# A deformable convolution with a ternary residual block: the head reordered, weight preparation moved, taps of the offset convolution levelled, x1 loaded two chunks ahead

## The reference

```
x = x + deform_conv(gn(x), w_off, b_off, w_conv)
x = x + block(gn(x), w1, gamma1, beta1, w2, gamma2, beta2)

deform_conv: om = conv3x3(y, w_off) + b_off        # 27 channels: 18 offsets, 9 masks
             for each of 9 taps: sample y bilinearly at the shifted place, times sigmoid(mask)
             out = sum over taps and channels with w_conv (256 x 256 x 9)
block:       out1 = relu(bn(conv3x3(y, ternary(w1))))
             out2 = bn(conv3x3(out1, ternary(w2)))
             out  = relu(out1 + out2)
ternary(w):  w - mean(w); -1 below min + third, +1 above max - third, else 0
```

## Time and profile before

| | |
|---|---|
| median of 3 runs | 2930.91 us (2930.48 to 2938.26) |
| the profiled execution | 2936.16 us, its span 2934.3 us |
| head, to VectorE's first chunk | 117.5 us |
| batch 0, chunks 0 to 7 | 574.0 us |
| batches 1 and 2 | 1054.9 us |
| batch 3 and the last chunk's end | 506.1 us |
| tail | 166.9 us |
| second block | 514.9 us |

### The profile page before, as it was taken

The page is one execution under the profiler, slowest core; times in us unless marked ns, Lnnn a source line. Parts: engine busy times, 40 slices in busy tenths (PEclk is TensorE's granted clock), DMA queues, the critical chain, the costliest instruction groups (busy, mean ns, idle before and its releaser), DMA issues. The chain is left out here.

```text
span 2934.3 us, 38779 instructions
## 1 busy us (share of the span) xinstructions
PE 2442.2 (83%) x12442; PEld 1692.3 (58%) x12442; DVE 2234.0 (76%) x4734; ACT 1275.2 (43%) x2181; POOL 1367.5 (47%) x1262
## 2 busy tenths in 40 slices
PE   4288888888999999999999998889887677999930
PEld 3144444444566566556566665555555677999930
DVE  6667777777888888888888887888786664666566
ACT  3244444445644445555555444444443123233245
POOL 1345554555655555556556555666652003333300
PEclk9699999999999999999999998999998888999975
DMA  7788888899999999999999999999995112111179
GB/s 248 270 292 301 317 304 303 311 348 353 332 360 354 360 351 351 342 329 363 337 361 363 343 330 325 345 347 343 342 343 218 50 61 70 53 60 52 44 278 408
DMA packets 277755, 826.29 MB, mean 282 GB/s; under 512 B 25692, under 2 KB 59484, under 8 KB 276964
## 3 DMA queue, kind: packets, MB, share of 16 engines
q0 software_dynamic: 165888, 604.05, 55.0%
q1 hardware_dynamic: 111716, 220.47, 21.7%
HBM read 738.95 MB, written 85.48 MB: 281 GB/s over the span
## 5 line engine op out<-in xcount | busy, mean ns | idle before, releaser
L447 POOL DMA_INDIRECT G<-pixel_pairs,quad_c x1152 | 1204.9, 1046 | 896.7 <-PE psT L1169 582.8
L961 DVE SCALAR_TENSOR_TENSOR G<-G,wts_c 128x256 f32<-128x256 f32 (+1 forms) x2304 | 1258.4, 612 | 217.5 <-DMA G<-pixel_pairs,quad_c 212.2
L1077 PE MATMUL psD<-ST,wconv 128*128 128x512 f32 x2304 | 1079.1, 613 | 0.0
L551 ACT ACTIVATE G<-G,wts_c 128x256 f32<-128x256 f32 x1152 | 490.5, 497 | 496.6 <-DVE G L961 496.5
L1077 PEld LDWEIGHTS psD<-ST,wconv 128*128 128x128 f32 x2304 | 434.6, 199 | 444.9 <-issue 444.9
L1169 PE MATMUL psT<-idn,G 128*128 128x128 f32 x2304 | 323.5, 286 | 218.8 <-ACT G L551 216.6
L607 ACT ACTIVATE ST<-psT 128x1024 f32<-128x1024 f32 x288 | 294.1, 1021 | 419.4 <-PE psT L1169 419.2
L1169 PEld LDWEIGHTS psT<-idn,G 128*128 128x128 f32 x2304 | 269.8, 146 | 314.7 <-ACT G L551 185.2
L1065 PE MATMUL psF<-pl,qw 128*128 128x256 f32 x1872 | 267.6, 298 | 35.7 <-DVE h1c L809 24.9
L1065 PEld LDWEIGHTS psF<-pl,qw 128*128 128x128 f32 x1872 | 244.2, 195 | 53.3 <-DVE h1c L809 21.2
L1046 PE MATMUL psA<-po,woff 128*64 128x512 f32 x864 | 253.2, 437 | 0.0
(11 more groups left out here) (214 smaller groups left out, 2241.0 us busy)
## 6 DMA issues: line engine op xcount, KB each, us to landing
xx<-in_x SPq DMA_DIRECT2D x56, 512.0 KB, 4.3
pixel_pairs<-yT SPq DMA_DIRECT2D x104, 256.0 KB, 7.2
G<-pixel_pairs,quad_c POOLq DMA_INDIRECT x1152, 6.6
x<-x1c SPq DMA_DIRECT2D x32, 512.0 KB
h<-h1c SPq DMA_DIRECT2D x32, 512.0 KB, 9.1
out<-h SPq DMA_DIRECT2D x16, 1024.0 KB, 17.3
xf<-x SPq DMA_DIRECT2D x24, 640.0 KB, 8.5
area<-h SPq DMA_DIRECT2D x24, 640.0 KB, 4.1
```

Source lines behind the costliest of these rows:

```text
L447: pool.indirect_dma_start(out=G[:, i % RING, :], out_offset=None, in_=tbl[d.b].rearrange("y x q c -> (y x) (q c)"), in_offset=bass.Indirec ...
L551: act.activation(g, g, ACT.Copy, scale=wts_c[:, d.p, i:i + 1]).then_inc(d_scaled, 1)
L961: dve.scalar_tensor_tensor(g[:, 0:w], g[:, w:2 * w], wts_c[:, d.p, q * NG + i:q * NG + i + 1], g[:, 0:w], ALU.mult, ALU.add).then_inc(d_ma ...
L1077: ins = pe.matmul(psD[:, oc, :], wconv[:, t, k, oc * 128:(oc + 1) * 128], ST[:, k % 3, t, :], start=(k == 0 and t == 0), stop=(k == TAPS - ...
```

## The change

It has five parts.

- SyncE's first loads: the two small constants that TensorE needs go first, then x of image 0, then the other constants. TensorE, ScalarE and VectorE no longer wait for all constants before they start; the offset weights are prepared after the moments (`offset_weights`).
- The head loses w1 (its 2.3 MB load and all work on it), the borders of tables 1 to 3, which go behind the last table write together with the load of w_conv, and the indices of chunk 1. The moments of image 1 read four buffers (all of xx) instead of two.
- w1 is loaded in six parts twice, once for its sums (VectorE at tap 3 of chunks 0, 3 and 4) and once for the comparison (chunks 6 and 7); its Winograd form is made at tap 7 of chunk 7.
- `O_TAPS` starts with one tap after k = 0 and ends after k = 4; `J_TAPS` moves to k = 5 to 8. The offset results of image s+1 are evacuated and turned one tap later, and both halves of their indices are made at k = 8. Those of image 0 are evacuated in the chunk behind, with the indices at k = 4 and 5.
- In the tail a chunk's load and `normalise` are done two chunks ahead. w2's sums are taken in chunks 4 and 5 of batch 3 from a load of their own; its ternary and Winograd forms are made by GpSimd in the tail. `load_w2`, `weight_sums` and `weight_limits` do for it what they do for w1.

```diff
-            xres, xz = xx[:, 0], [xx[:, 3], xx[:, 1]]
+            xres, xz = xx[:, 0], xx[:, 3]
...
+            w1_part = [xx[:, 1 + i].rearrange("p t x -> p (t x)")[:, 0:3 * C] for i in range(2)]
-            zero_sb = xf[:, 0, :, :, :].rearrange("p t h w -> p (t h w)")[:, 0:2 * C]
+            w2_part = [xo_flat[:, i * 3 * C:(i + 1) * 3 * C] for i in range(3)]
+            zero_sb = pl[:].rearrange("p q t r w -> p (q t r w)")[:, 3000:3000 + 2 * C].bitcast(F32)
...
-                    walk(eng, at, 5 if s == 0 else 3)
-            J_TAPS = {0: [0, 1], 1: [2, 3], 2: [4, 5], 3: [6, 7, 8]}
-            O_TAPS = {0: [0, 1, 2], 1: [3, 4], 2: [5, 6], 3: [7, 8]}
+                    walk(eng, at, 3 if 0 < s < NB - 1 else 5)
+            J_TAPS = {5: [0, 1], 6: [2, 3], 7: [4, 5], 8: [6, 7, 8]}
+            O_TAPS = {0: [0], 1: [1, 2], 2: [3, 4], 3: [5, 6], 4: [7, 8]}
...
+                def load_hz(r):
+                    if r >= 4:
+                        sp.wait_ge(z_stat, NR + CREDIT + r - 3)
+                    sp.dma_start(xx[:, r % 4], rows_of(x, 1, r * RC, RC)).then_inc(hz_load[r % 4], 16)
+
...
+                    for r in range(4):
+                        load_hz(r)
+                    load_j(Chunk(0, 2, 1, 0, False, False))
+                    sp.wait_ge(s_zero, 6)
+                    table_border(0, s_edge)
...
-                        if r == 1:
-                            sp.wait_ge(s_edge, 16 * 4 * NB)
-                            load_j(Chunk(0, 2, 1, 0, False, False))
-                        if 1 <= r < NR - 1:
-                            load_z(Chunk(1, r + 1, (r + 1) // 2, (r + 1) % 2, False, r + 1 == NR - 1))
-                        if r == 2:
-                            sp.dma_start(wconv[:].rearrange("p t k o -> p t (k o)"),
-                                         w_conv.rearrange("(t c) k o -> c t (k o)", c=128)).then_inc(s_wconv, 16)
...
+                        if r < 4:
+                            load_hz(r + 4)
+                        if r == 4:
+                            load_o(Chunk(1, 0, 0, 0, True, False))
+                    sp.dma_start(wconv[:].rearrange("p t k o -> p t (k o)"),
+                                 w_conv.rearrange("(t c) k o -> c t (k o)", c=128)).then_inc(s_wconv, 16)
+                    for b in range(1, NB):
+                        table_border(b, s_edge_rest)
+                    sp.wait_ge(z_stat, 2 * NR + CREDIT)
+                    load_w1(0)
...
-                    if f2:
+                    if f2 and (s < NB or f.first):
                         load_f(f2)
+                    if s == NB and f2 and not f2.last:
+                        load_f(f2.after())
...
+                        hold(sp, s_w2p, 3)
+                        load_w2(3)
...
+                    if s == 0 and d.is_row(6):
+                        sp.wait_ge(s_w1p, 8)
+                        load_w1(2)
...
+                        sp.wait_ge(s_w1p, 10)
+                        load_w1(4)
...
+                        for r, p0, done in ((0, 2, 2), (3, 4, 4), (4, 0, 6)):
+                            if d.is_row(r):
+                                sp.wait_ge(s_w1p, done)
+                                load_w1(p0)
...
+                def w2_ternary():
+                    pool.wait_ge(s_lim, 1)
+                    pool.wait_ge(s_wraw, 16)
+                    pool.tensor_scalar(above2, stage2, wall[:, 3:4], wall[:, 6:7], ALU.subtract, ALU.is_gt)
...
+                    g = [above2.rearrange("p (t y i) -> p t y i", t=CT, y=3)[:, :, y, :] for y in range(3)]
+                    both, minus = (stage2.rearrange("p (t y i) -> p t y i", t=CT, y=3)[:, :, y, :] for y in range(2))
+                    pool.tensor_tensor(both, g[0], g[2], ALU.add).then_inc(s_w2, 1)
...
+                    pool.tensor_scalar(minus, minus, 0.5, None, ALU.mult)
+                    pool.tensor_scalar(g[1], g[1], 0.5, None, ALU.mult).then_inc(s_tern, 1)
+
+                def emit(s, z, o, d, f, o2, f2, j, j2, fp, jp):
+                    if s == NB and f.first:
+                        w2_ternary()
...
-                            pool.wait_ge(s_edge, 16 * 4 * NB)
+                            pool.wait_ge(s_edge, 16 * 4)
...
+                        if f and f.first and not d and k == 1:
+                            planes_hi(s, f)
+                            normalise(f2, xf, f_load, sc1, bi1, f_y, None)
...
-                        if f2 and k == f_step(d, f):
+                        if f2 and d and k == f_step(d, f):
...
-                        if o and k == 4:
+                        if jp and k == 1:
+                            jt_om_evac(jp)
+                        if j and k == 1:
+                            jt_normalise(j)
+                        if jp and k == 3:
+                            jt_om_turned(jp)
+                        if o and k == 5:
                             om_evac(o)
...
+                    offset_weights()
                     dve.wait_ge(h_y, 2)
                     jt_split(j0, x_rows(0, 9))
-                    dve.wait_ge(s_w1, 48)
-                    weight_sums(0, raw1[0][3])
-                    take_stats(Chunk(1, 0, 0, 0, True, False))
-                    weight_sums(1, raw1[1][3])
-                    step(weight_sums(2, raw1[2][3]))
-                    weight_sums_ready(3)
+
...
+                        for t in range(CT):
+                            i = dve.bn_stats(st0[:, t, r, :], xx[:, r % 4, t, :])
...
-                    weight_extremes(0)
-                    weight_limits(0)
-                    compare_w1(0)
-                    take_stats(Chunk(1, 2, 1, 0, False, False))
-                    take_stats(Chunk(1, 3, 1, 1, False, False))
-                    compare_w1(1)
-                    compare_w1(2)
...
-                    winograd_w1()
-                    jt_split(j2, xf_rows(j2))
-                    jt_indices(j1, 0)
-                    jt_indices(j1, 1)
-                    for r in range(4, NR):
...
+                        if s == NB - 1 and k in (1, 3, 5) and (d.is_row(4) or d.is_row(5)):
+                            part = k // 2 + (3 if d.is_row(5) else 0)
+                            dve.wait_ge(s_w2l, 48 if d.is_row(4) else 96)
+                            weight_sums(part, w2_part[k // 2]).then_inc(s_w2p, 1)
...
-                        if o and k in (7, 8):
-                            o_indices(o, k - 7)
-                        if j and k in (7, 8):
-                            jt_indices(j, k - 7)
-                        if j2 and k == 7:
-                            jt_split(j2, xf_rows(j2))
+                        if o and k == 8:
+                            o_indices(o, 0)
+                            o_indices(o, 1)
+                        if j and k == 2:
+                            jt_split(j, xf_rows(j))
+                        if jp and k in (4, 5):
+                            jt_indices(jp, k - 4)
+                        if s == 0 and k == 3:
+                            for r, p0, loaded in ((0, 0, 32), (3, 2, 64), (4, 4, 96)):
+                                if d.is_row(r):
+                                    dve.wait_ge(s_w1, loaded)
+                                    for part in (p0, p0 + 1):
+                                        weight_sums(part, w1_part[part % 2]).then_inc(s_w1p, 1)
+                                    if r == 4:
+                                        dve.wait_ge(s_w1p, 6)
+                                        weight_sums_ready(6)
...
+                        if s == 0:
+                            for r, kk, p0, loaded in ((6, 1, 0, 128), (6, 6, 2, 160), (7, 6, 4, 192)):
+                                if d.is_row(r) and k == kk:
+                                    dve.wait_ge(s_w1, loaded)
+                                    compare_w1(p0)
+                                    compare_w1(p0 + 1)
+                        if s == 0 and k == 7 and d.is_row(7):
+                            dve.wait_ge(s_w1p, 12)
+                            winograd_w1()
...
                     if s == NB and f.first:
-                        dve.wait_ge(s_wraw, 16)
-                        step(weight_sums(0, stage2))
-                        weight_sums_ready(1)
...
+                    pe.wait_ge(s_const, 80)
+                    for r in range(3, 6):
+                        for tap in range(3 * (r - 3), 3 * (r - 2)):
+                            jt_conv(j0, tap)
+                        turn(r)
+                    turn(6)
                     jt_turn_om(j0)
...
+                    if s == 0 and d.is_row(5):
+                        pe.wait_ge(s_wtr, 2)
+                    if s == 0 and d.is_row(6):
+                        pe.wait_ge(s_lim1, 1)
...
+                            if k == 2 and jp:
+                                jt_turn_om(jp)
+                            if k == 6:
...
```

(27 more changed lines are left out.)

214 lines of the change are left out of this document (100 added, 114 removed).

## The result

| | before | after |
|---|---|---|
| median of 4 runs | 2934.59 us (2930.48 to 2940.38) | 2903.93 us (2900.94 to 2909.6) |
| the profiled execution, its span | 2936.16, 2934.3 us | 2900.94, 2899.2 us |

The ratio is 0.9898, with a 95% interval of 0.9880 to 0.9915. The direction was right; 2826 us was too fast by 78, and the result lies 42 us outside the range of 2797 to 2862.

A forecast was written before the change was run, and what follows sets the result against it. Batches 1 and 2 nearly fill TensorE, VectorE and DMA, batch 3 is DMA-bound; slack lies elsewhere. -40 - 26 + 0 + 7 - 46 = -105 on 2936.2 us gives 2831, the median 5.2 lower: 2826 us, range 2797 to 2862.

The forecast's parts named there:

- Head, -40: Start of the kernel: GpSimd starts at 70.1 us instead of 110.3, so -40 us; bounds -46 and -30.
- Batch 0, -26: Batch 0: levelled offset taps shorten chunks 1 to 5; sum 548 for 574 us, -26; bounds -42 and -5.
- a third shows: +7: Batch 0, chunks 6 and 7: of 21 us more VectorE work a third lengthens them, +7 us.
- Batches 1 and 2, 0: Batches 1 and 2: moved taps and index halves at tap 8 change the time by 0.
- the bounds that I gave: Batches 1 and 2: 1 us either way in each of 16 chunks.
- Same totals, other places: Batches 1 and 2: the work only moves between taps, its totals stay, so 0 us.
- The rival on late offsets: Batches 1 and 2: VectorE waits at tap 8, up to 7.3 us a chunk, batch 0 gains nothing: 2969 us; chance 0.03.
- Batch 3, +7: Batch 3: w2's second load costs 7 us, its sums are hidden or 8 us in part; bounds 0 and +15.
- Tail, -46: Tail: x1 two chunks ahead leaves TensorE the bound, six chunks at 12.2 us, -46 us; bounds -50 and -18.
- GpSimd's part: Tail: GpSimd's w2 passes take 19.9 us over two operands and 10 to 26 over one, from near 2284.
- ahead of the last matmul: Tail: GpSimd's w2 work ends between 2314 and 2331, before the last matmul.
- The first rival: Tail: GpSimd's SBUF passes stop VectorE's two-SBUF-operand plane operations; 28 us of gain lost, 2854 us; chance 0.23.

The follow-up runs named there:

- the early load: The changed kernel with the last two parts of w1 loaded ahead of chunk 7's table write in SyncE's queue, not behind it: 2900.53 us, one run.

## Why the prediction was wrong

**Head, -40: right, but for 3 us.** The rows show the steps as forecast: moments as x lands, then a queue that only writes and loads from 29.04 (forecast 28.7). Its writes and loads took 40.8 us instead of 37.6, and GpSimd starts 3.4 us later than forecast (73.5 for 70.1). No run undoes a part of the head by itself.

**Batch 0, -26: right in chunks 1 to 5, wrong at its end.** The step that failed is "a third shows: +7" for chunks 6 and 7. I counted VectorE's work on w1 and not a wait for its last load, which SyncE issues behind a wait of 25.9 us and a table write; VectorE stood 7.5 us for it. The chunks lost 17, and the early load gave 7.7 back in chunk 7; with it the two chunks still took 136.7 us, 11 above before for the 7 forecast. Chunk 0 took the full DMA (a share of 1.01 at 385 GB/s) and by its first multiply was still 6.6 us shorter (77.3 to 70.7).

**Batches 1 and 2, 0: wrong by 12 us,** within the bounds that I gave. "Same totals, other places" failed as a step: at a TensorE busy for 996 of 1055 us, the places cost too: with the older ones the batches took 1059.5 and 1061.2 us. The rival on late offsets named this place and asked for 5 us a chunk; it was 0.8, and by one profile most of it not from the indices that it blamed.

**Batch 3, +7: mis-sized, with the terms exchanged.** The sums, taken as hidden, cost about all of the 14 us: 18 reductions of 0.94 us, 17 us, on a VectorE that is busy for 50.4 of the 61 us of such a chunk before. The load, taken as the 7, cost nothing that one profile shows.

**Tail, -46: the main error, 44 of the 70 us between the forecast's 105 and the profile's 35.** Two things stood in the step on "GpSimd's part". Its ending "ahead of the last matmul" was taken as all that mattered, and the exclusion of VectorE given 0.23. And the passes were sized at 30 to 46 us and took 63.3: the four two-operand passes took 22.2 us for 19.9, near the forecast from the earlier trace rows (2.33 ns a column over 4608), but the comparison with two operations cost 3.45 ns (15.89 us for 4608), above my upper bound of 2.15. (VectorE worked beside these passes too, and no run has them alone, so how much of the 3.45 is theirs is open.) The first rival had the mechanism (an operation of the planes waits for a pass) and, with 28 us, the loss of the third chunk (27.23 us of TensorE's waiting). That this number fits is partly luck: it had all six operations of the planes wait, and only two did, for passes that were longer than thought. And GpSimd was still at work when the fourth chunk's planes came, and that chunk lost another 16.91. "SBUF — State Buffer" of the Trainium skill, section "Who interferes with whom", had named the effect, and the runs agree with it at every point they touch: a GpSimd pass that reads SBUF stretches a VectorE operation with both operands in SBUF (16.77 us for 2.50); the additions with one operand in PSUM keep their 0.41 us. My reason for giving it less weight, that a pass waiting for VectorE would cost nothing, counted only one of the two directions. That the gain of the two-ahead loads itself was right is shown by the tail of 97.3 us. From its first to its last matmul the forecast of -46 is 100 us (145.9 less 46; the 120 of the prediction counts from the end of the last deformable chunk). With GpSimd out and w2's limits ready, the chunks wait for next to nothing; the price is the 8 us by which w2's passes on VectorE then delay the second block.

## What to carry to other kernels

Before work is given to an idle GpSimd, look at which operands VectorE reads beside it: in the tail a pass over SBUF held a VectorE operation with both operands there until the pass was done, and as that engine was next to the bound, more was lost (44 us of TensorE's waits) than the passes cost on VectorE (16.5 us there, 63 on GpSimd). Such a loss is no wait of VectorE: it stands in the length of its instructions, and the list of waits names only VectorE's results, so compare the mean duration of a group before and after. And a load that is moved next to its user must be followed through the queue of its issuer: what stood ahead of it was not only 4 us of table write but the 25.9 us that the queue waits before it, and VectorE stood 7.5 us.

## What was not expected of the hardware

- The blocked time is inside the VectorE instruction's duration, from 677 ns to 14969 ns for the same instruction in the tail:

```profile
L828 DVE TENSOR_TENSOR xx<-xf x8: 677/3904/14969, 2252.3 to 2303.8; 128x512 f32<-128x512 f32 x8
```

- GpSimd's memsets, 17 in a row for 68.15 us (4.0 us for 4608 columns), cost the same VectorE operations nothing.
- In this trace one-operand GpSimd passes took longer than those over two operands: 15.89 us for two chained operations with limits per partition, against 10.73 for a subtraction of two tiles of the same size; the halving of 1536 columns took 4.41, the addition 3.83. All of them had VectorE operations beside them.
- After 27.23 us of idle time TensorE's next 24 matmuls took 4.63 us, after 16.91 us 4.81, where 3.10 is usual. The granted clock of the first 3 us of each is 0.50, the lower of its two levels (1.2 GHz), and 1.00 (2.4 GHz) behind them; it had fallen during the idle time. So each of these stalls costs TensorE 1.5 to 1.7 us more than its length.

```profile
2287.20:2290.20 3.00, 3.00 (x14) 3.00 (x15) 2.93 (x6) 0.00 (x0) 3.00 (x1) 0.50 0.02 7
2291.20:2299.00 7.80, 7.80 (x67) 7.80 (x66) 7.80 (x2) 0.00 (x0) 7.72 (x2) 1.00 0.34 104
```
